# Low parts of a two-layer graph network's first products: written by ScalarE and GpSimd in place of VectorE

## The chip, the cores and the metric

The kernel runs on one core of one Trainium2 chip. The metric is the device time of one execution, in microseconds, as the median of several runs. TensorE (PE) multiplies, VectorE (DVE), ScalarE (ACT) and GpSimd (POOL) do the elementwise work, SyncE (SP) starts most DMAs. GpSimd doesn't reach PSUM in this kernel: it reads and writes SBUF alone.

## The reference

Two graph networks in a row over 1250 nodes of 1024 features and 40000 edges. The change lies in the first:

```python
norm_x = t5_layer_norm(hidden_states, ln_weight)          # weight * x / sqrt(mean(x^2) + eps)
out = norm_x @ W_root + bias                              # 1024 -> 286
for r in range(2):
    w = (edge_type == r).astype(x.dtype)
    sums = segment_sum(norm_x[src] @ W_rel[r] * w[:, None], dst)
    out = out + sums / maximum(segment_sum(w, dst), 1.0)[:, None]
y = elu(out) @ wo_weight
x = layernorm(x + hidden_states + y)
```

The second network (a multilayer perceptron in, three layers of sums over neighbours, a decoder) follows; the change doesn't touch it.

## The kernel before

The 1250 nodes are ten tiles (T) of 125 rows. The first stage does two things side by side for each tile t.

**Products.** TensorE turns the tile's x in two halves of four transposes (`turn`, L730), ScalarE copies them to `xnT` with the norm's weight (`weigh`, L436), and TensorE multiplies by `w_all`, in eight steps u of two products of 429 columns (`products`, L736): 286 columns of W_root, 286 of each W_rel. The results lie in two PSUM banks, 2 + 2v and 3 + 2v, with v = t % 2. When they are complete, ScalarE (`evacuate`, L440 to L449) scales them by 1/rms and writes `y_root` (L447) and, rounded to the matmul's reduced format fp32r, `y_hi` in two pieces of 143 and 429 columns (L448, L449), and raises `y_copied`. VectorE (`low_part`, L1180 to L1188) then makes `y_lo`, the result times 1/rms less `y_hi`, read from PSUM again, in the same two pieces (L1186, L1187), and raises `y_split`. The next stage multiplies both parts by the adjacency.

**Counts.** The adjacency `adj` is counted from the edges, in groups of 500. For a group, VectorE builds two one-hot arrays in SBUF, `oh_low` (L1162) and `oh_code` (L1166), both from two inputs in SBUF; TensorE multiplies them in four products of 220 columns (`count`, L722); VectorE adds the result from PSUM into `adj` in two steps (`place`, L1194). There are two buffers: the one-hots of group g + 2 are built between the two additions of group g and behind them. A tile of the loop carries nine groups and eight product steps. So TensorE's order in a tile (`tile_of_1` of the tensor block) is: counts, then the products of step u, and so on; at u = 0 four transposes lie between them; at u = 4 four transposes and a second group, `row(5)`, lie between the counts and the products. VectorE's order (`tile_of_1` of the vector block) is the nine groups, at u = 3 the low part of tile t - 1 ahead of the group, at u = 5 a reciprocal for the norm (L1206). Tile 0 has products alone; tiles 1 to 8 run in a hardware loop of two tiles; tile 9 has eight groups and no double one.

TensorE waits at u = 0 for `y_split`, since the banks of tile t - 2 must be free, for `onehots` and `counts_free` at each group, and for `xnT_copied` at u = 0 and 4. The counters `y_copied` and `y_split` begin at 1 and 2. The next stage (`relations`) begins behind `y_split` of tile 8, and waits for that of tile 9 in front of the last tenth of its first sum (L880). GpSimd has in the first stage only `iota`s and two small writes of ones into `y_hi` (L368), then nothing until the encoder (L375).

`junk1`, which takes the squares that nobody reads, lies over the low parts of tiles 8 and 9; the staging arrays of the edges lie over those of 4 to 7 and over `y_root`.

Of the kernel before, what the change touches and what calls it, by code (L numbers as in the profile page):

```python
# [15 lines left out]
ALU = mybir.AluOpType  # L16
ACT = mybir.ActivationFunctionType
AX = mybir.AxisListType
F32 = mybir.dt.float32
# [6 lines left out]
P = 125  # L26
T = N // P
PM = P // 16 * 16
KD = D // 128
R, F = 2, 286  # L30
FW = 3 * F
FH = FW // 2
FA = F // 2
# [25 lines left out]
def graph_kernel(nc, x, src, dst, typ, ln_w, w_rel, w_root, conv_b, wo, g_in, b_in, w1, b1, w2, b2,  # L59
                 wa, ba, wb, bb, ng, nb, wd1, bd1, wd2, bd2, g_out, b_out, out):  # L60
    with ExitStack() as ctx:
        top = [16512]

        def at(off, name, shape, dt):
            return nc.alloc_sbuf_tensor_at(name, shape, dt, offset=off)

        def size(shape, dt):
            n = 2 if dt in (F16, BF16) else 4
            for k in shape[1:]:
                n *= k  # L70
            return -(-n // 32) * 32

        def stack(base, items):

            got = []
            for name, shape, dt in items:
                got.append(at(base, name, shape, dt))
                base += size(shape, dt)
            return got, base
# [8 lines left out]
            ("y_hi", [P, T, YH], F32R), ("y_lo", [P, T, 2 * F], F32R), ("y_root", [P, T, F], F32)])  # L88

        lo_base = y_base + size([P, T, YH], F32R)  # L90
        (junk1,), end = stack(lo_base + 8 * 4 * 2 * F, [("junk1", [P, D], F32)])
        assert end <= base - size([P, T, F], F32)
        (src_i, dst_i, typ_i, e_code, e_mark, bounds, lnw8, iota_r), end = stack(base - size([P, T, F], F32), [
# [264 lines left out]
        @block.gpsimd  # L358
        def _(pool):
            pool.iota(iota_r[:], [[1, 128]], base=0, channel_multiplier=0,  # L360
                      allow_small_or_imprecise_dtypes=True).then_inc(iotas, 1)
            pool.iota(iota_i[:], [[0, 1]], base=0, channel_multiplier=1,
                      allow_small_or_imprecise_dtypes=True).then_inc(iotas, 1)
            pool.wait_ge(small_set, 4)
            pool.iota(iota_c[:], [[16, R], [1, T], [32, W], [0, JH]], base=0, channel_multiplier=0,
                      allow_small_or_imprecise_dtypes=True).then_inc(iotas, 1)
            for c0 in (0, YH - 2):
                pool.tensor_scalar(y_hi[:, :, c0:c0 + 2], zero[:, 0:1].rearrange("p (a b) -> p a b", a=1).broadcast_to([P, T, 2]),  # L368
                                   1.0, None, ALU.add).then_inc(ones_set, 1)

            def second_norm(t):
                pool.wait_ge(ln2_shift, t + 1)
                if t >= 2:
                    pool.wait_ge(xhT_ps, 2 * t - 2)
                pool.tensor_scalar(xh[:, t % 2], x1(t), small2[:, 2, t:t + 1], small2[:, 3, t:t + 1],  # L375
                                   ALU.mult, ALU.add).then_inc(xh_ready, 1)

            def low_part(t, made):
                pool.wait_ge(hi_done, made)
                pool.tensor_tensor(h_lo[:, t], h[:, t], h_hi[:, t], ALU.subtract).then_inc(lo_done, 1)  # L380

            def with_bd2(t):

                pool.wait_ge(xh_ready, t + 1)
                pool.tensor_tensor(x1(t), x1(t), bd2_b[:], ALU.add).then_inc(xb_done, 1)

            pool.wait_ge(adj_sum, T)
            for t in range(4):
                second_norm(t)
            pool.wait_ge(fin_in, 48)  # L390
            pool.tensor_tensor(bo_b[:], bo_b[:], bd2_b[:], ALU.subtract).then_inc(bo_less, 1)
            for c in range(T // 2):
                for t in (2 * c + 4, 2 * c + 5):
                    if t < T:
                        second_norm(t)
                for t in (2 * c, 2 * c + 1):
                    low_part(t, t + 1)
                for t in (2 * c, 2 * c + 1):
                    with_bd2(t)
            with pool.Fori(1, L) as i:  # L400
                for t in range(T):
                    low_part(t, i * T + t + 1)


            pool.wait_ge(z_mm, L * len(CH))
            pool.wait_ge(bo_less, 1)
            pool.wait_ge(xb_done, T)
            for t in range(T):
                if t >= 2:
                    pool.wait_ge(o_res, t - 1)  # L410
                pool.tensor_tensor(x_bo[:, t % 2], x1(t), bo_b[:], ALU.add).then_inc(xo_done, 1)

        @block.scalar
        def _(act):
# [25 lines left out]
            def evacuate(t, v):  # L440

                wait_apart(act, proj_mm, 1 + t * 2 + 2)
                act.wait_ge(xn_rstd, t + 1)
                root, hi = y_root[:, bass.ds(t, 1)], y_hi[:, bass.ds(t, 1)]
                root, hi = root.rearrange("p o f -> p (o f)"), hi.rearrange("p o f -> p (o f)")
                rstd = small1[:, 4 + v:5 + v]
                act.activation(root, pb[0:P, 2 + 2 * v, 0:F], ACT.Copy, scale=rstd)  # L447
                act.activation(hi[:, 2:2 + FA], pb[0:P, 2 + 2 * v, F:FH], ACT.Copy, scale=rstd)  # L448
                act.activation(hi[:, 2 + FA:2 + 2 * F], pb[0:P, 3 + 2 * v, 0:FH], ACT.Copy, scale=rstd).then_inc(y_copied, 1)  # L449

            def tile_of_1(t, v, uses, last, cleared=None):
                act.wait_ge(xnT_ps, t * 2 + 2)
# [224 lines left out]
            for c in range(1, T // 2):  # L677
                t = 2 * c
# [30 lines left out]
        def _(pe):  # L709
# [31 lines left out]
            def tile_of_1(t, v, g0, odd, rows, uses):  # L741

                def row(r):
                    pe.wait_ge(onehots, g0 + r + 1)
                    pe.wait_ge(counts_free, g0 + r + 1)
                    count((odd + r) % 2).then_inc(counts_mm, 1)

                extra = rows - KD
                for u in range(KD):
                    row(u if u <= 4 else u + extra)  # L750
                    if u == 0:
                        pe.wait_ge(xnT_copied, 1 + t * 2)
                        turn(1, v)
                        pe.wait_ge(xnT_copied, 1 + t * 2 + 1)
                        pe.wait_ge(y_split, t + 1)
                    if u == 4:
                        pe.wait_ge(xnT_copied, 1 + t * 2 + 2)
                        if uses is not None:
                            pe.wait_ge(xs_in[1 - v], uses)
                            turn(0, 1 - v)  # L760
                        if extra:
                            row(5)
                    products(u, v)
# [310 lines left out]
        def _(dve):  # L1074
# [102 lines left out]
                    mini[0:1, bass.ds(g * H, H)], engines=[mybir.EngineType.DVE], min_val=0, max_val=N,  # L1177
                    skip_runtime_bounds_check_because="the least dst of a half row, and every dst is a node")[1]

            def low_part(t, v):  # L1180

                dve.wait_ge(y_copied, 1 + t + 1)
                hi, lo = y_hi[:, bass.ds(t, 1)], y_lo[:, bass.ds(t, 1)]
                hi, lo = hi.rearrange("p o f -> p (o f)"), lo.rearrange("p o f -> p (o f)")
                rstd = small1[:, 4 + v:5 + v]
                dve.scalar_tensor_tensor(lo[:, 0:FA], pb[0:P, 2 + 2 * v, F:FH], rstd, hi[:, 2:2 + FA], ALU.mult, ALU.subtract)  # L1186
                dve.scalar_tensor_tensor(lo[:, FA:2 * F], pb[0:P, 3 + 2 * v, 0:FH], rstd, hi[:, 2 + FA:2 + 2 * F],  # L1187
                                         ALU.mult, ALU.subtract).then_inc(y_split, 1)  # L1188

            def place(base, b, q, placed, done):  # L1190

                if placed:
# [5 lines left out]
            def tile_of_1(t, v, g0, odd, rows, placed):  # L1198

                base = bases(g0)  # L1200
                for u in range(rows):
                    if u == 3:
                        low_part(t - 1, 1 - v)
                    if u == 5:
                        dve.wait_ge(xn_sd, t + 1)
                        dve.reciprocal(small1[:, 4 + v:5 + v], small1[:, 2 + v:3 + v]).then_inc(xn_rstd, 1)  # L1206
                    g, b = g0 + u, (odd + u) % 2
                    dve.wait_ge(counts_mm, g + 1)
                    dve.wait_ge(counts_free, g + 2)
                    place(base, b, 0, placed, first_added)  # L1210
                    more = rows == UG or u + 2 < rows
                    if more:
                        lows(g + 2, b)
                    dve.wait_ge(first_added, g + 1)
                    place(base, b, 1, placed, counts_free)
                    if more:
                        codes(g + 2, b, edge[:, 1]).then_inc(onehots, 1)
                    if u + 1 < rows:
                        base = bases(g + 1)
# [34 lines left out]
            def after_counts():  # L1254

                dve.memset(small1[:, 7:8], 0.0).then_inc(adj_done, 1)
                low_part(T - 1, 1)
                dve.wait_ge(cb_in, 16)
                dve.wait_ge(y_copied, 1 + T)
                dve.memset(tails[:], 0.0).then_inc(tails_set, 1)  # L1260
                dve.wait_ge(tails_set, 1)
# [310 lines left out]
```

## Time and profile before

| | us |
|---|---|
| median of 3 runs | 589.47 |
| lowest, highest | 589.29, 590.37 |
| the profiled execution | 590.16 |
| its span, first to last instruction | 588.3 |
| PE busy | 572.2 (97%) |
| DVE busy | 385.1 (65%) |
| ACT busy | 223.7 (38%) |
| POOL busy | 88.6 (15%) |

A row of a timeline gives the start in us from the start of the span, the time it lasted, the engine, the line of the kernel, the operation, what it writes and reads, and in square brackets the engine's idle time in front of it with what ended it. A row "x4" is four instructions in a row. Matmuls overlap, so the distance from start to start says more than a row's length. A row of the waits is who waited for whom: us in total, how often, the longest.

### The profile page before, as it was taken

The page shows a single profiled execution, that of the slowest core. Times are in us where ns is not written, and L with a number is a line of the kernel's source. Part 1 is how long each engine was busy: PE and PEld are TensorE (multiplying, and loading weights), DVE is VectorE, ACT ScalarE, POOL GpSimd, SP SyncE. Part 2 cuts the span into 40 slices and gives each one's busy share as a digit, 9 for nine tenths or more (in the row PEclk, how much of TensorE's full clock was granted, in tenths as well). Part 3 has the DMA queues.
Part 4 walks back from the last instruction along what each step waited for, and adds up shares of the span by engine and source line. Part 5 has one row for each costly group of instructions (what it writes and reads, how often), then busy time and mean ns, then how long its engine had stood idle before and what let it go on. Part 6 is the DMA issues. An engine that isn't in the chain of part 4 may idle for free.

```text
span 588.3 us, 8363 instructions
## 1 busy us (share of the span) xinstructions
PE 572.2 (97%) x2584; PEld 396.1 (67%) x2584; DVE 385.1 (65%) x1000; ACT 223.7 (38%) x457; POOL 88.6 (15%) x70
## 2 busy tenths in 40 slices
PE   8999999999999999999999999999999999999992
PEld 4555555555577677675888888877877867455541
DVE  7598999888847888889503330018848657756455
ACT  5454344432213546553412221012223134276555
POOL 3000000000000000003065513401202230042230
PEclk9999999999999999999999999999999999999997
DMA  9510011111031112128300000600100100021123
GB/s 267 145 36 9 28 35 35 35 35 35 0 84 44 35 42 66 35 78 218 138 36 0 0 0 1 213 11 2 37 1 0 36 1 0 2 70 44 62 70 105
DMA packets 20871, 30.74 MB, mean 52 GB/s; under 512 B 5428, under 2 KB 15254, under 8 KB 20838
## 3 DMA queue, kind: packets, MB, share of 16 engines
q1 hardware_dynamic: 20422, 29.66, 17.1%
q10 hardware_dynamic: 416, 0.67, 0.4%
q8 instruction: 17, 0.28, 0.2%
q14 instruction: 16, 0.13, 0.1%
HBM read 25.20 MB, written 5.12 MB: 52 GB/s over the span
## 4 chain that ended last, share of the span: by engine, by line
PE 88%; DVE 4%; issue 2%; DVEq 2%; DMA 2%; ACT 1%; POOL 0%; SPq 0%
PE banks L736 16%; PE banks L935 12%; PE banks L1021 12%; PE banks L855 12%; PE banks L825 5%; PE banks L722 5%; PE banks L957 4%; PE banks L947 4%; PE banks L884 4%; PE banks L886 4%; PE banks L865 3%; PE banks L1011 3%; PE banks L829 2%; DVEq L1176 1%; PE banks L840 1%
## 5 line engine op out<-in xcount | busy, mean ns | idle before, releaser
L736 PE MATMUL banks<-w_all,xnT 128*125 128x429 f32 x320 | 130.3, 531 | 0.4 <-DMA w_all<-in_L_gnn_W_rel 0.4
L736 PEld LDWEIGHTS banks<-w_all,xnT 128*125 128x125 f32 x320 | 54.7, 190 | 30.7 <-issue 29.5
L1194 DVE TENSOR_TENSOR adj<-adj,banks 125x220 f32 x160 | 60.9, 381 | 17.5 <-PE banks L722 17.0
L855 PE MATMUL banks<-hT,w_s 128*128 128x250 f32 x320 | 68.7, 375 | 0.2
L855 PEld LDWEIGHTS banks<-hT,w_s 128*128 128x128 f32 x320 | 60.3, 190 | 8.9 <-issue 2.0
L884 PE MATMUL banks<-y_hi,adj 125*125 125x288 f32 x200 | 55.3, 304 | 0.6 <-issue 0.6
L722 PEld LDWEIGHTS banks<-oh_code,oh_low 125*128 125x128 bf16 x320 | 30.5, 97 | 35.1 <-issue 29.7
L886 PE MATMUL banks<-y_lo,adj 125*125 125x286 f32 x200 | 53.6, 295 | 0.0
L1340 DVE TENSOR_SCALAR hT<-banks,g_c,b_c 128x125 f32<-128x125 f32 x60 | 19.4, 400 | 45.1 <-PE banks L840 45.1
L1166 DVE TENSOR_TENSOR oh_code<-iota_c,edge 125x880 bf16<-125x880 f16 x80 | 48.9, 611 | 0.0
L935 PE MATMUL banks<-adj,h_hi 125*128 125x250 f32 (+1 forms) x180 | 48.2, 367 | 0.0
L375 POOL TENSOR_SCALAR xh<-x_first,small 125x1024 f32<-125x1024 f32 x6 | 7.4, 1241 | 260.2 <-DVE adj L1284 260.0
L722 PE MATMUL banks<-oh_code,oh_low 125*128 125x220 bf16 x320 | 44.7, 260 | 1.4 <-DVE oh_code L1166 0.9
L935 PE MATMUL banks<-adj,h_lo 125*128 125x250 f32 (+1 forms) x180 | 45.6, 353 | 0.0
L1021 PE MATMUL banks<-wd_s,dT 128*125 128x512 f32 x96 | 42.7, 592 | 0.0
L884 PEld LDWEIGHTS banks<-y_hi,adj 125*125 125x125 f32 x200 | 37.1, 186 | 7.4 <-issue 7.4
L380 POOL TENSOR_TENSOR h_lo<-h,h_hi 125x256 fp32r<-125x256 f32 x30 | 21.8, 733 | 108.0 <-ACT h_hi L571 108.0
L436 ACT ACTIVATE xnT<-banks,lnw 128x125 f32<-128x125 f32 x80 | 22.6, 376 | 40.5 <-PE banks L730 40.5
L886 PEld LDWEIGHTS banks<-y_lo,adj 125*125 125x125 f32 x200 | 37.4, 187 | 0.0
L825 PE MATMUL banks<-wo_s,yT 128*125 128x512 f32 x80 | 36.0, 592 | 0.0
L1162 DVE TENSOR_TENSOR oh_low<-iota_l,edge 125x512 bf16<-125x512 f16 x80 | 33.5, 419 | 0.2 <-issue 0.2
L935 PEld LDWEIGHTS banks<-adj,h_hi 125*128 125x128 f32 x180 | 29.8, 189 | 5.5 <-issue 1.4
(205 smaller groups left out, 878.3 us busy)
## 6 DMA issues: line engine op xcount, KB each, us to landing
xt<-in_x SPq DMA_DIRECT2D x15, 448.0 KB
out_x<-ot SPq DMA_DIRECT2D x9, 448.0 KB
w_s<-in_L_gnn_W SPq DMA_DIRECT2D x5, 512.0 KB, 6.1
xn<-in_x SPq DMA_DIRECT2D x5, 448.0 KB
wd_s<-in_L_gnn_Wd SPq DMA_DIRECT2D x1, 2048.0 KB, 13.7
w_all<-in_L_gnn_W_rel SPq DMA_DIRECT2D x6, 286.0 KB, 7.0
wo_s<-in_L_gnn_wo_weight SPq DMA_DIRECT2D x1, 1024.0 KB, 6.5
w_all<-in_L_gnn_W_root SPq DMA_DIRECT2D x3, 286.0 KB, 6.6
```

What stands on the lines that cost most here:

```text
L722: ins = pe.matmul(pb[:, b, q * R * C:(q + 1) * R * C], oh_low[:, b, q, :, j], oh_code[:, b, q, :, j], start=(j == 0), stop=(j == JH - 1))
L736: ins = pe.matmul(pb[0:P, 2 + 2 * v + n, 0:FH], xnT[:, u], w_all[:, u, n * FH:(n + 1) * FH], start=(u == 0), stop=(u == KD - 1))
L825: pe.matmul(pb[0:P, 5 + q], yT[:, i], wo_s[:, i, q * 512:(q + 1) * 512], start=(i == 0), stop=False)
L855: ins = pe.matmul(pb[:, 4 + f % 2, 0:2 * P], w1_s[:, k, f * 128:(f + 1) * 128], hT[:, k], start=(k == 0), stop=(k == KD - 1))
L884: pe.matmul(pb[0:P, b + r, 0:F + 2], mine, y_hi[:, s, r * (F + 2):(r + 1) * (F + 2)].bitcast(kind), start=(s == 0), stop=False)
L886: ins = pe.matmul(pb[0:P, b + r, w0:w0 + F], mine, y_lo[:, s, r * F:(r + 1) * F].bitcast(kind), start=False, stop=(s == T - 1))
L935: ins = pe.matmul(pb[:, 3 * f + c, 0:n], part[:, s, f * 128:(f + 1) * 128], adj[:, 0, s, c0:c0 + n], start=(s == 0 and part is h_hi), stop ...
L947: ins = pe.matmul(pb[:, 3 * f + c, 0:n], wa_s[:, k, f * 128:(f + 1) * 128], zT[:, k, c0:c0 + n], start=(k == 0), stop=(k == K2 - 1))
L1021: ins = pe.matmul(pb[0:P, 2 + 2 * u + q], (dT, dT_odd)[c % 2][:, k, u * P:(u + 1) * P], wd2_s[:, k, q * 512:(q + 1) * 512], start=(k == 0) ...
L1162: return dve.tensor_tensor(oh_low[:, b], both(iota_l, LOW), spread_out(edge[:, 0], g, LOW), ALU.is_equal)
L1166: return dve.tensor_tensor(oh_code[:, b], both(iota_c, R * C), spread_out(code, g, R * C), ALU.is_equal)
L1194: dve.tensor_tensor(cols, cols, window(b, q), ALU.add).then_inc(done, 1)
```

## The change

ScalarE's `evacuate` also writes the results scaled but not rounded to a new array `y_f`, which lies on the same bytes as `y_lo`, in two further activations of 143 and 429 columns; `y_copied` is raised behind them. GpSimd subtracts `y_hi` from `y_f` into `y_lo`, in place, one instruction of 572 columns for each of the ten tiles, and raises `y_split`. VectorE's `low_part` is gone. TensorE's wait at u = 0 and a wait of VectorE in front of its reciprocal (which overwrites the 1/rms that ScalarE has read) are on `y_copied` in its place.

```diff
         lo_base = y_base + size([P, T, YH], F32R)
+        y_f = at(lo_base, "y_f", [P, T, 2 * F], F32)
...
+            for t in range(T):
+                pool.wait_ge(y_copied, 1 + t + 1)
+                pool.tensor_tensor(y_lo[:, t], y_f[:, t], y_hi[:, t, 2:2 + 2 * F], ALU.subtract).then_inc(y_split, 1)
+
             def second_norm(t):
...
                 act.activation(hi[:, 2:2 + FA], pb[0:P, 2 + 2 * v, F:FH], ACT.Copy, scale=rstd)
-                act.activation(hi[:, 2 + FA:2 + 2 * F], pb[0:P, 3 + 2 * v, 0:FH], ACT.Copy, scale=rstd).then_inc(y_copied, 1)
+                act.activation(hi[:, 2 + FA:2 + 2 * F], pb[0:P, 3 + 2 * v, 0:FH], ACT.Copy, scale=rstd)
+                whole = y_f[:, bass.ds(t, 1)].rearrange("p o f -> p (o f)")
+                act.activation(whole[:, 0:FA], pb[0:P, 2 + 2 * v, F:FH], ACT.Copy, scale=rstd)
+                act.activation(whole[:, FA:2 * F], pb[0:P, 3 + 2 * v, 0:FH], ACT.Copy, scale=rstd).then_inc(y_copied, 1)
...
                         pe.wait_ge(xnT_copied, 1 + t * 2 + 1)
-                        pe.wait_ge(y_split, t + 1)
+                        pe.wait_ge(y_copied, t)
...
-            def low_part(t, v):
-
-                dve.wait_ge(y_copied, 1 + t + 1)
-                hi, lo = y_hi[:, bass.ds(t, 1)], y_lo[:, bass.ds(t, 1)]
-                hi, lo = hi.rearrange("p o f -> p (o f)"), lo.rearrange("p o f -> p (o f)")
-                rstd = small1[:, 4 + v:5 + v]
-                dve.scalar_tensor_tensor(lo[:, 0:FA], pb[0:P, 2 + 2 * v, F:FH], rstd, hi[:, 2:2 + FA], ALU.mult, ALU.subtract)
-                dve.scalar_tensor_tensor(lo[:, FA:2 * F], pb[0:P, 3 + 2 * v, 0:FH], rstd, hi[:, 2 + FA:2 + 2 * F],
-                                         ALU.mult, ALU.subtract).then_inc(y_split, 1)
-
...
-                    if u == 3:
-                        low_part(t - 1, 1 - v)
                     if u == 5:
+                        dve.wait_ge(y_copied, t)
                         dve.wait_ge(xn_sd, t + 1)
...
-                low_part(T - 1, 1)
```

VectorE in the loop, where the third group of a tile ends and the next begins (u = 2 to u = 3), before:

```order
L1166 TENSOR_TENSOR oh_code<-iota_c,edge 125x880
L1176 ISA
L1176 TENSOR_LOAD mini
L1186 ISA [waits y_copied]
L1186 REGISTER_ALU
L1186 SCALAR_TENSOR_TENSOR y_lo<-banks,small_88,y_hi 125x143
L1187 ISA
L1187 SCALAR_TENSOR_TENSOR y_lo<-banks,small_88,y_hi 125x429
L1209 REGISTER_ALU [waits counts_mm]
L1194 ISA [waits counts_free]
L1194 TENSOR_TENSOR adj<-adj,banks 125x20x11
```

The same place now:

```order
L1174 TENSOR_TENSOR oh_code<-iota_c,edge 125x880
L1184 ISA
L1184 TENSOR_LOAD mini
L1206 REGISTER_ALU [waits counts_mm]
L1192 ISA [waits counts_free]
L1192 TENSOR_TENSOR adj<-adj,banks 125x20x11
```

The two low-part instructions are gone, and the wait for the counts follows the one-hots directly.

ScalarE at the end of a tile in the loop, now (before, the copies into `xnT` followed the second activation on `y_hi`):

```order
L452 ACTIVATE y_root<-banks,small_89 125x286
L453 ISA
L453 ACTIVATE y_hi<-banks,small_89 125x143
L454 ISA
L454 ACTIVATE y_hi<-banks,small_89 125x429
L456 ISA
L456 ACTIVATE y_f<-banks,small_89 125x143
L457 ISA
L457 ACTIVATE y_f<-banks,small_89 125x429
L460 ISA
L461 REGISTER_ALU [waits xnT_ps]
L441 ACTIVATE xnT<-banks,lnw 128x125 [waits proj_mm]
```

The two activations on `y_f` are new, and the next tile's copies stand behind them.

## Rows read from the trace of the kernel before

**Rows 1.** The page's head.

```profile
span 588.3 us, 8363 instructions
```

**Rows 2.** Waits of the first stage, 0 to 180 us.

```profile
ACT xnT L436 <- PE banks L730: 40.5, 10, 4.9
...
DVE adj L1194 <- PE banks L722: 17.0, 37, 2.7
...
PEld banks L722 <- DVE oh_code L1166: 4.9, 16, 0.5
```

**Rows 3.** Timeline of PE in tile 3: S0, first products, S1, S4, S5.

```profile
56.08 0.56 PE L722 MATMUL banks<-oh_code,oh_low 125*128 125x220 bf16 x4
...
56.90 1.61 PE L736 MATMUL banks<-w_all,xnT 128*125 128x429 f32 x4
58.34 0.56 PE L722 MATMUL banks<-oh_code,oh_low 125*128 125x220 bf16 x4
...
63.89 0.56 PE L722 MATMUL banks<-oh_code,oh_low 125*128 125x220 bf16 x4
...
64.99 0.57 PE L722 MATMUL banks<-oh_code,oh_low 125*128 125x220 bf16 x4
```

**Rows 4.** Timeline of PE, S5 of tile 1 and S5 of tile 8.

```profile
32.16 0.57 PE L722 MATMUL banks<-oh_code,oh_low 125*128 125x220 bf16 x4
...
146.83 0.56 PE L722 MATMUL banks<-oh_code,oh_low 125*128 125x220 bf16 x4 [0.20 <-DVE oh_code L1166]
```

**Rows 5.** Timeline of DVE in tile 3, 58 to 66 us.

```profile
58.13 0.61 DVE L1166 TENSOR_TENSOR oh_code<-iota_c,edge 125x880 bf16<-125x880 f16 x1
...
59.43 0.42 DVE L1162 TENSOR_TENSOR oh_low<-iota_l,edge 125x512 bf16<-125x512 f16 x1
...
61.91 0.61 DVE L1166 TENSOR_TENSOR oh_code<-iota_c,edge 125x880 bf16<-125x880 f16 x1
62.54 0.37 DVE L1186 SCALAR_TENSOR_TENSOR y_lo<-banks,small,y_hi 125x143 f32 x1
62.83 0.66 DVE L1187 SCALAR_TENSOR_TENSOR y_lo<-banks,small,y_hi 125x429 f32 x1
63.40 0.38 DVE L1194 TENSOR_TENSOR adj<-adj,banks 125x220 f32 x1
...
64.32 0.61 DVE L1166 TENSOR_TENSOR oh_code<-iota_c,edge 125x880 bf16<-125x880 f16 x1
```

**Rows 6.** Timeline of ACT behind tile 2's products.

```profile
56.81 0.37 ACT L448 ACTIVATE y_hi<-banks,small 125x143 f32 x1
57.07 0.62 ACT L449 ACTIVATE y_hi<-banks,small 125x429 f32 x1
57.57 1.14 ACT L436 ACTIVATE xnT<-banks,lnw 128x125 f32<-128x125 f32 x4
```

**Rows 7.** Lines L380 and L411 on POOL: ns min/median/max, first and last start.

```profile
L380 POOL TENSOR_TENSOR h_lo<-h,h_hi x30: 722/733/742, 298.0 to 469.0; 125x256 fp32r<-125x256 f32 x30
...
L411 POOL TENSOR_TENSOR x_bo<-x_first,bo_b x6: 2346/2351/2369, 473.1 to 534.3; 125x1024 f32<-125x1024 f32 x6
```

**Rows 8.** Timeline of ACT and PE, end of the stage and the aggregation's 37th product.

```profile
170.34 0.62 ACT L449 ACTIVATE y_hi<-banks,small 125x429 fp32r<-125x429 f32 x1
...
175.12 0.29 PE L884 MATMUL banks<-y_hi,adj 125*125 125x288 f32 x1
```

**Rows 9.** Line L1437 on DVE, and timeline of DVE and POOL at 467 us.

```profile
L1437 DVE SCALAR_TENSOR_TENSOR zt<-zt,small,nb_b x30: 483/485/1026, 401.3 to 508.2; 125x256 f32<-125x256 f32 x30
...
466.98 1.03 DVE L1437 SCALAR_TENSOR_TENSOR zt<-zt,small,nb_b 125x256 f32<-125x256 f32 x1
...
467.00 0.73 POOL L380 TENSOR_TENSOR h_lo<-h,h_hi 125x256 fp32r<-125x256 f32 x1 [2.41 <-ACT h_hi L571]
```

**Rows 10.** Timeline of ACT and DVE in tile 1.

```profile
25.02 0.62 ACT L449 ACTIVATE y_hi<-banks,small 125x429 fp32r<-125x429 f32 x1
...
26.58 0.42 DVE L1162 TENSOR_TENSOR oh_low<-iota_l,edge 125x512 bf16<-125x512 f16 x1
```

## The prediction

> **What bounds the kernel now.** First the page's head: the profiled execution spans 588.3 us [rows 1] and took 590.16 us, so 1.9 us lie around the span; the median of the three runs, 589.47 us, is 0.7 us below that execution. The change touches the first stage alone, from about 23 us to 170 us, so I ask who waits for whom there [rows 2]. VectorE waits 17.0 us for TensorE's counts (L722), and TensorE's weight loads wait 4.9 us for VectorE's one-hots (L1166). Both can't be the bound at once: TensorE leads nearly everywhere, and at some places VectorE is late. Those places are what a lighter VectorE can win, so the next view is TensorE's own timeline.
>
> In tile 3 of the loop [rows 3] I write S0 to S8 for the starts of its nine groups of counts, S5 being the one that the code calls row(5). S0 to S1 is 58.34 - 56.08 = 2.26 us (with four transposes in it), S1 to S4 is 63.89 - 58.34 = 5.55 us (three steps of 1.85 us), and the four steps from S5 to the next S0 are of the same kind, 7.40 us. All of these run at TensorE's own pace. Between S4 and S5 there are only four counts and four transposes, no products. The same two pieces took 56.90 - 56.08 = 0.82 us at S0; here they took 64.99 - 63.89 = 1.10 us. So TensorE stalls about 0.28 us in front of S5, the one place where it asks for two sets of one-hots in quick succession. A tile without a stall would take 2.26 + 5.55 + 0.82 + 7.40 = 16.03 us. From S5 of tile 1 to S5 of tile 8 [rows 4] there are seven tiles in 146.83 - 32.16 = 114.67 us, 16.38 us each. **The stalls in front of S5 are therefore 0.35 us per tile, 114.67 - 7 x 16.03 = 2.46 us in all.**
>
> Who makes TensorE wait there? The timeline of VectorE in the same tile [rows 5]. The group at S2 = 58.34 + 1.85 = 60.19 has its one-hots done at 61.91 + 0.61 = 62.52, S2 + 2.33. From its first addition to there a group takes 1.53 us (63.40 to 64.32 + 0.61 = 64.93, next group), so VectorE can begin one at S + 0.80. For S3 = 63.89 - 1.85 = 62.04 that would be 62.84; but the low part starts at 62.54, and the addition comes only at 63.40, 0.56 us late. The one-hots for S5 end at 64.93, and S5 is 64.99, 0.06 us behind. Released, they would end at S3 + 2.33 = 64.37 us, and S5 could be had at S4 + 0.82 = 64.71. **The margin would be 64.71 - 64.37 - 0.06 = 0.28 us.**
>
> **The change, part by part.**
>
> *VectorE loses the two instructions at its third group* in each of the nine loop tiles, and the pair behind the loop. From rows 5 they hold it for 63.40 - 62.54 = 0.86 us per tile. By the margin above all of the stall in tiles 2 to 8 goes: -2.46 us. The tenth tile has no double row, so there is nothing to win in it. The pair behind the loop counts for nothing: VectorE's next work there is on the first aggregation, and TensorE is in its products until after 175.12 us [rows 8].
>
> *ScalarE writes the results twice.* Two activations of the same shapes as those of lines 448 and 449 are added. The gaps from start to start give 57.07 - 56.81 = 0.26 us, and from the last one to the next instruction 57.57 - 57.07 = 0.50 us [rows 6]: 0.76 us per tile, 7.6 us over ten, all on ScalarE. It costs nothing, since ScalarE waited 40.5 us for TensorE's transposes in front of its next copies (L436) [rows 2], ten times, about 4 us each. What queues behind: the copies for products u = 4 to 7, which now end about 57.57 + 1.14 + 0.76 = 59.5 us in tile 3, and are wanted behind the counts of S4, at 63.89 + 0.40 = 64.3 us. The signal y_copied comes at 57.07 + 0.62 + 0.76 = 58.45 us. TensorE's new wait for it (u = 0) is for the results of the tile two before, signalled 2.4 us after the S0 of the tile before, 16.38 - 2.4 = 14 us ago; VectorE's new wait in front of its reciprocal asks for the same signal later still.
>
> *GpSimd subtracts*, ten instructions of 572 elements on 125 partitions. There is no such row. The same kind took 0.733 us for 256 elements and 2.351 us for 1024 [rows 7]; between them that is 0.733 + 316 x (2.351 - 0.733) / 768 = 1.40 us. I take 1.40 and keep 0.73 and 2.35 as ends. GpSimd is idle in this stage. TensorE needs the last one at the 37th product of the next stage, at 175.12 us [rows 8]; ScalarE's signal comes at 170.34 + 0.62 + 0.76 = 171.72 us, and with 0.06 us for a semaphore, as above, and 1.40 us GpSimd is done at 173.2 us, 1.9 us early.
>
> *The port between GpSimd and VectorE* is where a new wait can arise. In the layers a VectorE instruction with both inputs in SBUF (L1437) lasts 0.485 us; one that was issued at 466.98 us, when GpSimd's subtraction had taken hold (467.00 to 467.73), lasted 1.03 us and so was held back until 467.53 [rows 9]. So such an instruction waits for GpSimd's, until about 0.2 us before the end of its record. Both one-hot instructions (L1162, L1166) are of this kind; the additions take one input from PSUM. In tile 3 GpSimd would be ready at 58.45 + 0.06 = 58.51 us, where L1166 (58.13 to 58.74) has the port, so it starts at 58.74 and releases at 58.74 + 1.40 - 0.20 = 59.94 us. L1162, due at 59.43, is then late by d = 0.51 us. TensorE has 1.85 us from group to group and a VectorE that is behind needs 1.53 us, so it regains 0.32 us per group, 0.64 us over the two groups up to S3. With the margin of 0.28 us: **stall per tile = d - 0.92, nothing for d = 0.51.** The cost is 0 here. For GpSimd's lower end (0.73 us) it is 0 too. For the upper end (2.35 us) d = 58.74 + 2.15 - 59.43 = 1.46 us and the stall is 0.54 us, 0.19 us more than the 0.35 us of now.
>
> In tile 1 GpSimd comes at a worse moment: y_copied at 25.02 + 0.62 + 0.76 = 26.40, GpSimd at 26.46, just ahead of L1162 at 26.58 [rows 10]. It holds until 26.46 + 1.20 = 27.66, d = 1.08 us, a stall of 0.16 us. Put at the others' 0.35 us of now, it might win 0.2 us; since the start hangs on 0.1 us, I count no gain (ends 0 and -0.35 us).
>
> The Trainium skill speaks against the move: GPSIMD Engine Reference, section Engine selection, puts elementwise work on VectorE, since GpSimd is about twice as slow with two inputs. Taken from the 0.37 + 0.66 = 1.03 us that VectorE's pair lasts [rows 5], that would be an estimated 2.05 us on GpSimd, d would be 1.16 us, the stall 0.24 us per tile, and only 0.8 us would be won. I keep the 1.40 us from the rows of GpSimd itself.
>
> **Sum:** -2.46 + 0 (ScalarE) + 0 (port) + 0 (tile 1). The profiled execution goes from 590.16 to 587.7 us, and, as the runs' median is 0.7 us below it, the median to 589.47 - 2.46 = **587.0 us**. Everything behind the stage is chained to its end, the loads for the next stage too, and moves with it. A measurement of this kernel tells about 0.2%, 1.2 us, from no change.
>
> **Rivals.**
> 1. *No change: the port gives back what VectorE saves.* Place: L1162 of the second group, or of the third if GpSimd is a group later. With GpSimd taking hold just ahead of L1162 in every tile, as in tile 1, d is 1.40 - 0.20 = 1.20 us, the stall 0.28 us instead of 0.35: 589.0 us. For it: GpSimd's start hangs on ScalarE, and in the third group the regained time is only 0.32 us. Against: the start, 58.74, is 0.7 us off that worst moment in tile 3. Up to d = 0.92 nothing is lost, so only a late start within the last 0.3 us ahead of L1162 costs anything. The Trainium skill says it outright: Perfetto Trace Analysis, section Optimizing Scalar/DVE Operations, says offloading between these two might not help, because they share a read port. No row of the first stage shows it, since GpSimd is idle there.
> 2. *Slower: GpSimd holds the port too long.* Place: the same. It decides from a d of 0.92 + 0.35 = 1.27 us, that is from an instruction of about 2.2 us on GpSimd. With 2.35 us it costs 7 x 0.19 = 1.3 us, and in tile 1 d is 26.46 + 2.15 - 26.58 = 2.03, its stall 1.11 instead of 0.35, 0.8 us more: 589.47 + 2.1 = 591.6 us. For it: the one-hots keep the port 1.0 of 1.85 us, and GpSimd's read could be interrupted. Against: its subtractions lasted 722 to 742 ns in all 30 cases [rows 7].
> 3. *The change doesn't do what it says: TensorE's stall at S5 is not VectorE's.* Going from transposes to counts could cost 0.3 us by itself. Then nothing changes, 589.5 us. Against: S5 follows the one-hots by 0.06 us.
>
> **How the numbers follow.** Forecast 0.67, rival 1 0.19, rival 2 0.07, rival 3 0.07. The forecast's own range: 2.8 us (with tile 1) off the lowest run, 589.29, gives 586.5; 587.7 at the other end. To leave out no more than 2 in 10 it reaches into rival 1, up to 589.2. Faster by over 0.2%: the forecast and the better part of rival 1, 0.74. Same: the rest of rival 1 and rival 3, 0.19. Slower: 0.07.
>
> **What would show it.** Right: S4 to S5 is 0.82 us in tiles 2 to 8, the seven tiles take 112.2 us, GpSimd's rows last 1.3 to 1.5 us, one L1162 or L1166 (new numbers) per tile lasts longer by some 0.5 us, and no wait of TensorE for one-hots is left but in tile 1. Wrong: S4 to S5 stays at 1.1 us or more (which one-hot record is long then tells rival 1 or 2; none, rival 3), or the stage ends 2.5 us earlier and a later wait takes it back, the DMA of cb_b ahead of the first aggregation before all.

## The result, and the profile after

The changed kernel takes 586.85 us (median of 22 runs, 586.35 to 589.53), the kernel before beside it 589.82 us (22 runs, 589.23 to 592.06). The ratio is 0.9958, with a 95% interval of 0.9947 to 0.9968: 0.42% faster, 2.5 us by the ratio and 3.0 us by the medians. The forecast was 587.0 us. The profiled execution took 587.64 us.

The head of the page of the changed kernel:

```profile
span 585.8 us, 8370 instructions
...
PE 570.0 (97%) x2584; PEld 395.6 (68%) x2584; DVE 379.7 (65%) x980; ACT 231.6 (40%) x477; POOL 100.7 (17%) x80
```

ScalarE gained 7.9 us of work, GpSimd 12.1 us, VectorE lost 5.4 us (the low part gone, its waits for the port added). TensorE's busy time fell by 2.2 us without one instruction less, which is why busy time doesn't answer the question. TensorE's timeline in tile 3 does (start, length, as in [rows 3]: S0, the first products, S1, S4, S5):

```profile
55.86 0.56 PE L730 MATMUL banks<-oh_code,oh_low 125*128 125x220 bf16 x4
...
56.68 1.61 PE L744 MATMUL banks<-w_all,xnT 128*125 128x429 f32 x4
58.12 0.56 PE L730 MATMUL banks<-oh_code,oh_low 125*128 125x220 bf16 x4
...
63.67 0.56 PE L730 MATMUL banks<-oh_code,oh_low 125*128 125x220 bf16 x4
...
64.49 0.56 PE L730 MATMUL banks<-oh_code,oh_low 125*128 125x220 bf16 x4
```

S0 to S1 is 2.26 us and S1 to S4 5.55 us, both as before; S4 to S5 is 0.82 us where it was 1.10. The first and the last S5 of the loop's tiles, against [rows 4]:

```profile
32.43 0.56 PE L730 MATMUL banks<-oh_code,oh_low 125*128 125x220 bf16 x4
...
144.65 0.56 PE L730 MATMUL banks<-oh_code,oh_low 125*128 125x220 bf16 x4
```

They lie 112.22 us apart, 7 x 16.03, and were 114.67 us apart. All eight gaps S4 to S5 are 0.82 or 0.83 us, and no other distance between groups of counts is longer than at its own pace: in the loop nothing holds TensorE up any more.

VectorE in the same tile, against [rows 5], from the one-hots of S0 to those made for S5:

```profile
57.89 0.61 DVE L1174 TENSOR_TENSOR oh_code<-iota_c,edge 125x880 bf16<-125x880 f16 x1
58.91 0.39 DVE L1192 TENSOR_TENSOR adj<-adj,banks 125x220 f32 x1 [0.41 <-PE banks L730]
59.21 0.62 DVE L1170 TENSOR_TENSOR oh_low<-iota_l,edge 125x512 bf16<-125x512 f16 x1
...
62.61 0.38 DVE L1192 TENSOR_TENSOR adj<-adj,banks 125x220 f32 x1 [0.31 <-PE banks L730]
...
63.54 0.61 DVE L1174 TENSOR_TENSOR oh_code<-iota_c,edge 125x880 bf16<-125x880 f16 x1
```

The one-hots for S5 end at 64.15, S3 + 2.33 (S3 = 61.82), and TensorE takes them at 64.49 in its own time. One oh_low lasts 0.62 us in place of 0.42, and it is the one that meets GpSimd's instruction. ScalarE and GpSimd around it:

```profile
56.85 0.62 ACT L454 ACTIVATE y_hi<-banks,small 125x429 f32 x1
57.35 0.39 ACT L456 ACTIVATE y_f<-banks,small 125x143 f32 x1
57.62 0.64 ACT L457 ACTIVATE y_f<-banks,small 125x429 f32 x1
58.12 1.16 ACT L441 ACTIVATE xnT<-banks,lnw 128x125 f32<-128x125 f32 x4
```

```profile
58.33 1.23 POOL L374 TENSOR_TENSOR y_lo<-y_f,y_hi 125x572 fp32r<-125x572 f32 x1 [14.41 <-ACT y_f L457]
```

ScalarE's two activations take 58.12 - 57.35 = 0.77 us, and GpSimd starts 0.07 us behind them. Over all ten tiles the source lines of GpSimd and of oh_low read (ns, least, median, longest):

```profile
L374 POOL TENSOR_TENSOR y_lo<-y_f,y_hi x10: 1197/1198/1227, 27.1 to 169.6; 125x572 fp32r<-125x572 f32 x10
```

```profile
L1170 DVE TENSOR_TENSOR oh_low<-iota_l,edge x80: 410/418/1402, 20.1 to 162.7; 125x512 bf16<-125x512 f16 x80
```

The source line of oh_low in the kernel without GpSimd's subtraction (e4, below) has no long record at all, so the long ones are GpSimd's doing:

```profile
L1166 DVE TENSOR_TENSOR oh_low<-iota_l,edge x80: 416/418/425, 19.0 to 161.6; 125x512 bf16<-125x512 f16 x80
```

In each of the nine tiles behind the first, one oh_low was held, by 0.09 to 0.98 us. The longest is in tile 1 (timeline of VectorE and of GpSimd, against [rows 10]):

```profile
27.15 1.40 DVE L1170 TENSOR_TENSOR oh_low<-iota_l,edge 125x512 bf16<-125x512 f16 x1
```

```profile
27.07 1.20 POOL L374 TENSOR_TENSOR y_lo<-y_f,y_hi 125x572 fp32r<-125x572 f32 x1 [19.50 <-ACT y_f L457]
```

GpSimd came 0.08 us ahead and VectorE lost 1.40 - 0.42 = 0.98 us, with no stall behind it.

**Where 2.5 us of span went.** By the starts on TensorE's timelines: tile 1, S0 to S5, 8.94 to 8.64 us, -0.30; tiles 2 to 8, -2.45; from S5 of tile 8 to the last counts, -0.01; from there to the first product of the aggregation, 2.65 to 2.17 us, -0.48; from there to the first product with wo, 11.34 to 11.63 us, +0.29; the rest of the kernel -0.12. That is -3.07 us from S0 of tile 1 to the end. The first 23 us, which the change doesn't touch, were 0.57 us longer (S0 at 23.79 in place of 23.22). The first product started 0.45 us later, when its weights had arrived, and the first eight products took 0.12 us more from start to start. Both parts move from one profiled execution to the next. The rows of the kernel before, of the changed one, and of e6 and e7 below (timelines of TensorE, the first eight products):

```profile
8.41 4.70 PE L736 MATMUL banks<-w_all,xnT 128*125 128x429 f32 x8 [0.36 <-DMA w_all<-in_L_gnn_W_rel]
```

```profile
8.86 4.81 PE L744 MATMUL banks<-w_all,xnT 128*125 128x429 f32 x8 [1.92 <-DMA w_all<-in_L_gnn_W_rel]
```

```profile
9.10 6.00 PE L737 MATMUL banks<-w_all,xnT 128*125 128x429 f32 x8 [1.17 <-DMA w_all<-in_L_gnn_W_rel]
```

```profile
9.34 3.12 PE L746 MATMUL banks<-w_all,xnT 128*125 128x429 f32 x8 [1.59 <-DMA w_all<-in_L_gnn_W_rel]
```

The next eight take 3.09 us in all four. What makes the first eight longer isn't shown.

### The profile page after: what moved, and what is told of

It is laid out like the page before. It is cut to its first block, busy times and chain, and to the rows that moved or that the text cites. A ratio compares the mean times of both kernels' runs of the same rounds, so it can differ in the third digit from the quotient of the medians.

```text
span 585.8 us, 8370 instructions
## 1 busy us (share of the span) xinstructions
PE 570.0 (97%) x2584; PEld 395.6 (68%) x2584; DVE 379.7 (65%) x980; ACT 231.6 (40%) x477; POOL 100.7 (17%) x80
## 4 chain that ended last, share of the span: by engine, by line
PE 94%; DMA 2%; DVE 2%; ACT 1%; POOL 0%; SPq 0%; issue 0%
PE banks L744 20%; PE banks L943 12%; PE banks L1029 12%; PE banks L863 12%; PE banks L730 5%; PE banks L833 5%; PE banks L965 4%; PE banks L955 4%; PE banks L892 4%; PE banks L894 4%; PE banks L873 3%; PE banks L1019 3%; PE banks L837 2%; PE banks L848 1%; PE banks L738 1%; DMA cb_b<-in_L_gnn_conv_bias 1%
## 5 line engine op out<-in xcount | busy, mean ns | idle before, releaser
L374 POOL TENSOR_TENSOR y_lo<-y_f,y_hi 125x572 fp32r<-125x572 f32 x10 | 12.0, 1201 | 151.2 <-ACT y_f L457 151.2
L1170 DVE TENSOR_TENSOR oh_low<-iota_l,edge 125x512 bf16<-125x512 f16 x80 | 36.6, 457 | 0.2 <-issue 0.2
```

What stands on the lines that cost most here:

```text
L1170: return dve.tensor_tensor(oh_low[:, b], both(iota_l, LOW), spread_out(edge[:, 0], g, LOW), ALU.is_equal)
```

## The experiments

My theory: the whole gain is the stall in front of S5; the stall depends on how late VectorE is at the group before, and GpSimd's hold of the port is paid by VectorE where there is time to regain it. The rivals: it is VectorE's total load; it is ScalarE's part or the end of the stage; GpSimd's place doesn't matter. Eight kernels, in two sets, each with the kernel before timed beside it (589.67 us in the first set, 589.84 us in the second). Since S0 of tile 1 moved between 22.7 and 25.2 us from one profiled execution to the next (the first product's start and the first eight products, as above), I also give the distance from there to the end of the span, which is free of it. The last two columns are each from one profiled execution.

| kernel | median us | ratio (95%) | S5 of tile 1 to S5 of tile 8 | S0 of tile 1 to the end |
|---|---|---|---|---|
| before | 589.82 | | 114.67 | 565.08 |
| changed | 586.85 | 0.9958 (0.9947 to 0.9968) | 112.22 | 562.01 |
| e1_low_at_1 | 587.55 | 0.9960 (0.9947 to 0.9972) | 112.21 | 562.22 |
| e2_double_1 | 588.85 | 0.9988 (0.9979 to 0.9997) | 113.97 | 564.30 |
| e3_pool_at_3 | 590.83 | 1.0015 (1.0004 to 1.0026) | 115.01 | 565.38 |
| e4_no_subtract | 587.16 | 0.9956 (0.9943 to 0.9969) | 112.22 | 562.09 |
| e5_act_only | 589.74 | 0.9994 (0.9978 to 1.0010) | 114.67 | 564.92 |
| e6_nobody | 587.29 | 0.9948 (0.9928 to 0.9968) | 112.22 | 562.28 |
| e7_pool_at_2 | 586.97 | 0.9955 (0.9939 to 0.9972) | 112.24 | 562.26 |
| e8_low_at_4 | 590.07 | 1.0004 (0.9991 to 1.0017) | 114.48 | 564.83 |

### Only the place moved: e1_low_at_1

```diff
                 for u in range(rows):
-                    if u == 3:
+                    if u == 1:
                         low_part(t - 1, 1 - v)
```

> The kernel before with VectorE's low part in front of the second group of a tile (u = 1) in place of the fourth (u = 3). My theory: the whole gain comes from the stall in front of S5, and only the place of the 0.86 us matters. At u = 1 the low part begins at about S1 + 0.4 (behind the one-hots of S0), makes the group 0.47 us late, and 0.64 us is regained by S3: no stall, S4 to S5 0.82 us in tiles 1 to 8, and the time of the changed kernel, 587.0 us, with a ratio of 0.995 to 0.996. Rival (VectorE's total load, or the end of the stage, counts): VectorE does as much as before, so 589.8 us, ratio 1.000.

Measured: 0.9960, eight gaps S4 to S5 of 0.82 or 0.83 us, and 112.21 us over the seven tiles. VectorE does all that it did before, two groups earlier, and the gain is the same within the intervals. VectorE's load as the cause falls; so do TensorE's and VectorE's changed waits for `y_copied`, which this kernel doesn't have. In VectorE's timeline the low part starts behind the one-hots of S0, and the addition of the second group follows it at 59.47:

```profile
58.61 0.37 DVE L1186 SCALAR_TENSOR_TENSOR y_lo<-banks,small,y_hi 125x143 f32 x1
58.90 0.65 DVE L1187 SCALAR_TENSOR_TENSOR y_lo<-banks,small,y_hi 125x429 f32 x1
59.47 0.37 DVE L1194 TENSOR_TENSOR adj<-adj,banks 125x220 f32 x1
...
62.69 0.38 DVE L1194 TENSOR_TENSOR adj<-adj,banks 125x220 f32 x1
```

The addition of the group at S3 (61.91) begins at 62.69, S3 + 0.78: what was late is regained in two groups.

### The load at the good place doubled: e2_double_1

```diff
...
-                    if u == 3:
+                    if u == 1:
                         low_part(t - 1, 1 - v)
+                        dve.bn_stats(spare[:, 0:6], pb[0:P, 2 + 2 * (1 - v), F:FH])
+                        dve.bn_stats(spare[:, 6:12], pb[0:P, 3 + 2 * (1 - v), 0:FH]).then_inc(bound_off, 1)
```

> As e1_low_at_1, and behind the low part two statistics instructions on the same PSUM columns (143 and 429), whose results nobody reads: some 0.8 us more for VectorE at u = 1. By the arithmetic the group is 0.47 + 0.8 = 1.27 us late, 0.64 us is regained by S3 and 0.28 us is margin: a stall of 0.35 us in front of S5 in each of 8 tiles, so 589.7 us, ratio 1.000. Rival (a place early in the tile hides any such load): 587.0 us. Second rival (TensorE stalls at S3 already, where it would want the one-hots at S1 + 3.70): over 591 us.

Measured: 0.9988, between the two times expected (mine was 1.000). The stall is back in front of S5 and nowhere else: the gaps are 1.00 to 1.24 us, the seven tiles 1.75 us more than in the changed kernel, 0.25 us each, where I had worked out 0.35. The place hides a load only up to a size. The first rival falls, the second too (S1 to S4 stays at 5.54 to 5.55 us). Of the missing 0.10 us per tile, 0.07 is that low part and statistics together took 1.59 us (75.01 to 76.60) and not the 0.86 + 0.8 = 1.66 that I had assumed.

### VectorE's low part one group later: e8_low_at_4

```diff
-                    if u == 3:
+                    if u == 4:
                         low_part(t - 1, 1 - v)
```

> The kernel before with VectorE's low part at u = 4 in place of u = 3. Theory: the one-hots for S5 are then on time (S4 to S5 0.82 us) but those for S6 end at S4 + 2.33 + 0.54 = S4 + 2.87, wanted at S4 + 2.67: a stall of 0.26 us moves to between S5 and S6 (2.11 us in place of 1.85), 0.8 us in all less than before, about 589.0 us, ratio 0.999. Rival (only the gap in front of S5 is tight): the changed kernel's time, ratio 0.995.

Measured: a ratio of 1.0004 (0.9991 to 1.0017), so the small gain that I expected (0.8 us, 0.999) didn't show. In the trace S0 to the end is 0.25 us shorter than before, and the seven tiles 0.19 us. The place of the stall came out as expected: S4 to S5 is 0.82 or 0.83 us in all eight tiles, and S5 to S6 has become 2.11 to 2.21 us, where it was 1.85 or 1.86. In the tile at 63 us (timeline of TensorE: S4, the transposes, S5, products, S6):

```profile
63.33 0.56 PE L722 MATMUL banks<-oh_code,oh_low 125*128 125x220 bf16 x4
63.73 0.59 PE L730 MATMUL banks<-ident,xt 125*128 125x125 f32 x4
64.15 0.56 PE L722 MATMUL banks<-oh_code,oh_low 125*128 125x220 bf16 x4
64.55 1.61 PE L736 MATMUL banks<-w_all,xnT 128*125 128x429 f32 x4
66.27 0.57 PE L722 MATMUL banks<-oh_code,oh_low 125*128 125x220 bf16 x4
```

The stall moved one gap on. It is 0.27 us here, as worked out (0.26), but 0.35 or 0.36 us in the even tiles, which is why most of the expected gain is missing; why even and odd tiles differ isn't shown. The gap S4 to S5 isn't slow by itself: the stall goes with VectorE's low part.

### GpSimd at the bad place: e3_pool_at_3, and one group earlier: e7_pool_at_2

```diff
             for t in range(T):
                 pool.wait_ge(y_copied, 1 + t + 1)
+                if t < T - 1:
+                    pool.wait_ge(counts_mm, t * UG + 3 + 1)
```

and, for e7, the same with `+ 2 + 1`.

> The changed kernel, but GpSimd's subtraction for a tile also waits for the counts of the fourth group (u = 3) of the next tile. Theory (port): GpSimd starts at S3 + 0.63 and keeps oh_low's instruction (due S3 + 1.08) waiting until S3 + 1.69; 0.61 us late with a margin of 0.28 us gives a stall of 0.33 us in front of S5 in 8 tiles, 2.6 us: 589.5 us, ratio 0.999 to 1.000, with one L1170-type record of about 1.0 us per tile. Rival (no port wait that matters, or the changed kernel's gain does not hang on where GpSimd works): 587.0 us, ratio 0.995.

> The changed kernel, with GpSimd's subtraction also waiting for the counts of the third group (u = 2). Theory (port, stall = delay less what is regained): in e3_pool_at_3 the instruction held back lost 0.67 us and TensorE stalled 0.39 us, 0.28 us less. One group earlier 0.32 us more is regained, so the stall is 0.07 us per tile, S4 to S5 0.89 us, 0.6 us in all. Rival (GpSimd anywhere but at its own place costs about what it did in e3): S4 to S5 1.2 us.

Measured, e3: 1.0015, slower than the kernel before, with the gain gone and the stall at 0.38 to 0.41 us in each of the eight tiles. Its tile 3, on GpSimd, VectorE and TensorE:

```profile
63.86 1.19 POOL L376 TENSOR_TENSOR y_lo<-y_f,y_hi 125x572 fp32r<-125x572 f32 x1 [15.23 <-PE banks L732]
```

```profile
64.25 1.09 DVE L1172 TENSOR_TENSOR oh_low<-iota_l,edge 125x512 bf16<-125x512 f16 x1
...
65.56 0.60 DVE L1176 TENSOR_TENSOR oh_code<-iota_c,edge 125x880 bf16<-125x880 f16 x1
```

```profile
65.01 0.56 PE L732 MATMUL banks<-oh_code,oh_low 125*128 125x220 bf16 x4
65.41 0.59 PE L740 MATMUL banks<-ident,xt 125*128 125x125 f32 x4
66.22 0.57 PE L732 MATMUL banks<-oh_code,oh_low 125*128 125x220 bf16 x4 [0.22 <-DVE oh_code L1176]
```

oh_low's record starts at 64.25, GpSimd's goes from 63.86 to 65.05, and oh_low ends at 65.34. With its usual 0.42 us it ran from 64.92, 0.13 us before the end of GpSimd's record. It lost 1.09 - 0.42 = 0.67 us; the one-hots end at 66.16 and S5 is 66.22, 1.21 us behind S4. The stall is 0.39 us, which is 0.67 less the margin of 0.28. I had expected 0.61 us lost, 0.33 us of stall, and at worst the time of the kernel before; 0.39 us is more than the 0.35 us of before, hence the ratio above 1. The same three engines do the same work as in the changed kernel; only the moment differs, and it is worth 3.4 us between the two kernels (565.38 - 562.01).

Measured, e7: oh_low loses the same 0.67 us (1.09 us at 60.23), but one group earlier, and all gaps are 0.82 or 0.83 us: 0.9955. I had expected 0.07 us of stall per tile. VectorE regained 0.39 us and not 0.32: behind a group that was held back, the next addition starts 0.53 us behind its oh_code (61.54 to 62.07), elsewhere 0.61. The one-hots then end at 63.60 and S5 is at 63.66 in TensorE's own time, which is the limit to a hundredth. VectorE's timeline there:

```profile
60.23 1.09 DVE L1172 TENSOR_TENSOR oh_low<-iota_l,edge 125x512 bf16<-125x512 f16 x1
...
61.54 0.60 DVE L1176 TENSOR_TENSOR oh_code<-iota_c,edge 125x880 bf16<-125x880 f16 x1
62.07 0.37 DVE L1194 TENSOR_TENSOR adj<-adj,banks 125x220 f32 x1
...
62.99 0.61 DVE L1176 TENSOR_TENSOR oh_code<-iota_c,edge 125x880 bf16<-125x880 f16 x1
```

### What is free: e4_no_subtract, e5_act_only, e6_nobody

e4 leaves out the subtraction, so the next stage sums other numbers: GpSimd's loop is gone, ScalarE's two activations write to the bytes of `y_lo`, and the next stage waits for `y_copied`. e5, on the kernel before:

```diff
         lo_base = y_base + size([P, T, YH], F32R)
+        y_f = at(lo_base, "y_f", [P, T, 2 * F], F32)
...
-                act.activation(hi[:, 2 + FA:2 + 2 * F], pb[0:P, 3 + 2 * v, 0:FH], ACT.Copy, scale=rstd).then_inc(y_copied, 1)
+                act.activation(hi[:, 2 + FA:2 + 2 * F], pb[0:P, 3 + 2 * v, 0:FH], ACT.Copy, scale=rstd)
+                whole = y_f[:, bass.ds(t, 1)].rearrange("p o f -> p (o f)")
+                act.activation(whole[:, 0:FA], pb[0:P, 2 + 2 * v, F:FH], ACT.Copy, scale=rstd)
+                act.activation(whole[:, FA:2 * F], pb[0:P, 3 + 2 * v, 0:FH], ACT.Copy, scale=rstd).then_inc(y_copied, 1)
```

e6, on the changed kernel: neither the subtraction nor the two activations, waits on `y_copied` in the next stage, and there

```diff
-                            ins = pe.matmul(pb[0:P, b + r, w0:w0 + F], mine, y_lo[:, s, r * F:(r + 1) * F].bitcast(kind),
+                            ins = pe.matmul(pb[0:P, b + r, w0:w0 + F], mine, y_hi[:, s, 2 + r * F:2 + (r + 1) * F].bitcast(kind),
```

> The changed kernel without GpSimd's subtraction: ScalarE writes the unrounded results where the low parts lie, and TensorE's waits in the next stage are on ScalarE's signal. Left out: the subtraction, so the sums are of other numbers. Theory: GpSimd's ten instructions cost nothing in the changed kernel, 586.9 us, ratio 0.995, within 0.2 us of the changed kernel. Rival (the port costs some tiles part of the gain): lower by up to 0.5 us.

> The kernel before, with ScalarE's two further activations per tile (to the bytes where the low parts lie) ahead of its signal; VectorE keeps its low part at u = 3. Theory: ScalarE's 0.76 us per tile are free and win nothing, so S4 to S5 stays at 1.10 to 1.19 us and the time at 589.7 us, ratio 1.000. Rival (part of the changed kernel's gain or cost is ScalarE's): a ratio off 1.000 by more than 0.001.

> No engine makes a low part: VectorE's, ScalarE's two activations and GpSimd's subtraction are all left out, and the next stage multiplies the high part twice. Left out: the low parts. Theory: the stage is then as TensorE alone can do it, and the changed kernel was there already: from the first counts to the end of the span 562.0 us as in the changed kernel, ratio 0.995 to 0.996. Rival (ScalarE or the port still costs something): 0.5 us or more below the changed kernel from the same point.

Measured: e4 and e6 have the changed kernel's 112.22 us to the hundredth, and 562.09 and 562.28 us from S0 to the end beside its 562.01. So neither GpSimd's nor ScalarE's work costs anything there, and with no low part at all nothing more is won: TensorE's own order of work sets the loop's time. e5 has the kernel before's 114.67 us and gaps, and 0.9994 with 1 inside the interval: ScalarE's part neither wins nor costs. No run pointed to a version faster than these; e1 reaches the changed kernel's time with one number edited.

## Why the prediction was right, point by point

- **The number.** 587.0 us forecast, 586.85 measured; that they are so close is in part luck. The forecast took 2.46 us off a median of three runs, 589.47 us; the 22 runs beside the changed kernel have 589.82, and the drop is 3.0 us by the medians, 2.5 us by the ratio. Of the 3.07 us from S0 to the end, 2.45 are the stalls of tiles 2 to 8, 0.30 tile 1, and 0.3 lie behind the loop, the last two forecast as nothing. In the profiled execution, 587.64 us against the 587.7 forecast, the 0.57 us of the start made up for them.
- **The stall in front of S5, 2.46 us in tiles 2 to 8, all of it to go.** Measured 114.67 - 112.22 = 2.45 us. That VectorE's low part at u = 3 made it is shown by e1 (moved, and gone) and e8 (moved, and behind it). Rival 3 (0.07) falls.
- **The margin of 0.28 us.** e3 gives 0.67 - 0.39 = 0.28 us, and the changed kernel 64.49 - 64.15 - 0.06 = 0.28 us.
- **ScalarE: 0.76 us per tile, hidden.** 0.77 us, and e5 shows it free.
- **GpSimd: 1.40 us.** Mis-sized: 1.20 us. The straight line between 256 and 1024 elements [rows 7] was too high for 572. The two rows aren't quite of one kind: the 256 are a subtraction written as fp32r, like the new one, the 1024 an addition written as fp32. Whether that or the size bends the line isn't tested. The last subtraction ended at 170.83 us, 1.6 us before the 37th product (172.45). The estimate by twice VectorE's time, 2.05 us (the Trainium skill, GPSIMD Engine Reference, section Engine selection) was further off: 1.20 against 1.03 us, a factor of 1.16.
- **The port: starts at 58.74, d = 0.51 us, no stall.** The wait came where it was put, and the sizes were smaller: oh_low lost 0.62 - 0.42 = 0.20 us. The tile began 0.22 us earlier in this trace, so 58.74 is 58.52 here, and GpSimd was recorded from 58.33: oh_code, recorded to 58.50, hardly held it (GpSimd's record is 0.03 us longer than in the other tiles). That is 0.19 us off d, the shorter instruction another 0.17, and the release 0.15 us before the end of the record, where I had taken 0.20, adds 0.05. The other tiles were not alike: between 0.09 and 0.98 us were lost, by when GpSimd started.
- **Rival 1, the port gives it back,** had its place wrong. I had put the danger at an oh_low of the second group, with 0.28 us of stall for the worst moment. Tile 1 was that moment, with the shorter instruction (0.98 us lost, where I allowed for 0.92), and had no stall at all; e7 shows that one held group regains 0.39 us and not 0.32. The danger is real two groups later: e3 loses all of the gain, and the interval of 1.0004 to 1.0026 is above 1. The page of the Trainium skill that warns that offloading between GpSimd and VectorE might not help (Perfetto Trace Analysis, section Optimizing Scalar/DVE Operations) describes e3; the changed kernel is the case where it helps, because the held instruction is one that had time.
- **Rival 2** needed about 2.2 us on GpSimd; the ten took 1.20 to 1.23 us.
- **Tile 1, counted as no gain:** 0.30 us won, inside the ends given.
- **Everything behind moves along:** from the last counts to the end of the span it was 0.3 us less (-0.48 + 0.29 - 0.12). The 0.48 us lie before the first aggregated product, where TensorE had stood idle 0.64 us with no releaser in the profile, and then 0.16 us. That distance, last counts to first aggregated product, is 2.17 to 2.84 us over the ten profiled kernels, and the next part gives back what it wins (11.63 to 11.05 us to the first product with wo), because the DMA of cb_b, started at the end of the stage, is on the chain to that point (6.19 us before, 6.00 us now, which is the 0.19 us that the two parts together won). What the 0.64 us are is open.
- **"No wait of TensorE for one-hots left"** was wrong as a sign to look for. The waits of the first stage still have

```profile
PEld banks L730 <- DVE oh_code L1174: 3.5, 17, 0.2
```

  3.5 us in 17 waits of the weight loads, against 4.9 us in 16 [rows 2], though the stalls went from 2.8 us to nothing. A weight load can wait beside running products and delay nobody; the distance from start to start is what counts.

## What to carry to other kernels

Where one engine leads and another keeps just behind, look for the one place where the leader asks twice in quick succession, and measure the gap there against the same work elsewhere in its own timeline. That difference, and not the time that leaves the follower, is what a lighter follower wins. Then ask for the place before the amount: here the same 0.86 us of VectorE cost 0.35 us per tile at u = 3, 0.32 us at u = 4 ((114.48 - 112.22) / 7), and nothing at u = 1. Work given to GpSimd beside VectorE instructions with two SBUF inputs was free two groups ahead of the tight one, just free one group ahead, and took back all that it saved in the tight group itself.

## What the runs showed of the hardware

A one-hot instruction of VectorE, both inputs in SBUF, waits for a running subtraction of GpSimd, to 0.13 to 0.15 us before the end of its record, and its own record contains the wait (0.42 us became 0.62, 1.09 and 1.40 us, by when GpSimd had started; without the subtraction, in e4, the longest of 80 is 0.425 us). The other way round little was seen: GpSimd's record began 0.17 us before the end of an oh_code record and was 0.03 us longer, and twice 0.08 us before it and was no longer. GpSimd's subtraction of 572 fp32 elements lasted 1.20 us, where one of 256 took 0.73 and an addition of 1024 took 2.35. And the start of the loop moved between 22.7 and 25.2 us over ten profiled kernels, nearly as much as the change is worth: the first product, which waits for its weights, started at 8.39 to 10.05 us, and the first eight products took 3.12 to 6.00 us. With a gain of 0.4%, the distances inside the stage say more than a single span.
